# Scores as three f16 products, one product for the last key, and another order of steps in a Perceiver block on one Trainium2 core

## The chip, the core and the metric

The kernel runs on one core of one Trainium2 chip. Four engines take part, each with its own instruction queue: TensorE (PE, matmuls into PSUM), VectorE (DVE), ScalarE (ACT) and GpSimd (POOL); SyncE (SP) issues most of the transfers. The metric is the device time of one execution in microseconds (us), the median of several runs.

## What is computed

The reference takes 64 sequences of 32 tokens (width 256) with 64 contexts of 257 keys (width 128), and adds three layers to the tokens, each behind a layer norm: cross attention, self attention with ternary weights, and a mixture of 8 experts with a capacity of 256 rows each.

```python
x = x + _L0_xattn_ref(_layernorm(x, axis=-1), ctx_1024, Wq, Wk, Wv, Wo, gq, gk)
x = x + _L0_attn_ref(_layernorm(x, axis=-1), w_qkv, w_proj, q_gain)
x = x + _L0_ffn_ref(_layernorm(x, axis=-1), Wg, W1, W3, W2, sw1, sw3, sw2)
# cross attention, 16 heads of width 128
q = rmsnorm((hidden_states @ Wq).reshape(B, Sq, H, D), gq)
k = rmsnorm((encoder_hidden_states @ Wk).reshape(B, Skv, H, D), gk)
scores = jnp.einsum('bqhd,bkhd->bhqk', q, k) * scale
attn = jax.nn.softmax(scores, axis=-1)
out = jnp.einsum('bhqk,bkhd->bqhd', attn, v)
```

## The kernel before

Four sequences (128 tokens) make a tile, and there are 16 tiles. The program is a prologue, a loop of 15 turns, a last part and the experts. A turn of the loop does the cross attention of the next tile up to its probabilities, and everything behind it (the two other layers) of the tile before. The prologue prepares the weights and does the first tile's cross attention; the last part does the late steps of tile 15.

The work of a turn is cut into named steps. Each engine runs its steps in the order of a list (`ORDER`, in the prologue `START_ORDER`), and semaphores tie them: `filled[bank]` counts what TensorE has put in a PSUM bank, `drained[bank]` what has been taken out of it, and a step that writes a bank waits until the one before it there is drained. So the lists and the banks set the order. PSUM is four banks of AB (slots 0 to 3), two of C (4 and 5), Db (D) and Eb (E).

The steps that matter here, with b the sequence of the tile (0 to 3):

- `K0` to `K7`: the keys, of which only the squared norms are wanted. TensorE writes four banks with three products each of f16 halves (`wk_hi`, `wk_lo`, `c_hi`, `c_lo`; high part and remainder). ScalarE squares banks 0 and 1 (`square_keys`, L961), VectorE takes statistics of banks 2 and 3 (`key_stats`, L1345). `KN`, `gKN` and `kn` turn the sums of four steps into inverse norms: VectorE, ScalarE (a logarithm and an exponential as a first guess), VectorE.
- `h` (GpSimd) splits a sequence's context into halves for `K`; `c` and `cl` do so with the rows for `o`.
- `f` closes the cross attention of the tile before (48 products), `Q` makes the queries for their norms (`RQ`, `gRQ`, `rq`), `QP` makes queries times keys' weights, 96 products of f16 halves. ScalarE copies `QP` from AB to `qpT` in f32 (L970) and so drains its banks.
- `rk` (GpSimd, TensorE, ScalarE) spreads the keys' inverse norms, `s` makes the scores: TensorE multiplies `qpT` by `ctxT` in f32, four products of 257 columns (`scores`, L734 to L737), VectorE scales them and takes their maximum (L1513). `e` is the exponential on ScalarE (L1031), `i` the inverse of its sum on VectorE, `n` the normalisation on GpSimd (L1202 to L1212).
- `pt` turns the probabilities on TensorE (`turn_probs`, L739 to L749). The last key doesn't fit in the two blocks of 128; its probabilities stand in `plast`, a row of 12 for each of 4 head groups, and four products with a unit matrix turn them into Db. ScalarE (`ph`, `tl`) and VectorE (`dp`) drain; `o` multiplies with the context rows, `oh` and `do` drain it.
- self attention of the tile before: `xt1`, `qkv`, `gqkv`, `qr` (VectorE, ending with `heads`), `qk` (TensorE turns the heads, ScalarE copies them), `sc` (64 small products), `sm`, `pv`, `st`, `y`, `ys`, `yv`, `pr`; then `ln2`, `xt2`, `lg`, `up`, `dn`, `pos` and `scat`, which sends the rows to the experts.

Of the kernel before, what the change touches and what calls it, by code (L numbers as in the profile page):

```python
# [1791 lines left out]
```

## Time and profile before

| what | value |
|---|---|
| median of 3 runs | 1457.01 us (1456.34 to 1458.7) |
| profiled execution: its time as span | 1457.0 us |
| TensorE busy | 1274.8 us, 87% |
| VectorE busy | 916.5 us, 63% |
| ScalarE busy | 892.3 us, 61% |
| GpSimd busy | 541.9 us, 37% |
| mean granted TensorE clock | 0.954 of full speed |
| prologue, loop, rest | about 0 to 122, 122 to 1277, 1277 to 1457 us |

In a timeline row the columns are the start in the span, the length, the engine, the line of the program, the operation, what is written and read with its shape, and the count; in brackets stands how long the engine sat idle before it and what ended that. A TensorE row's length runs to the end of the pipelined product, so rows overlap and the distance between two starts is what a product costs.

### The profile page before, as it was taken

How to read it: one execution, taken by the hardware profiler on the slowest of the kernel's cores; microseconds unless marked ns; L12 is line 12 of the kernel's file. 1: busy time of each engine (PE TensorE's matmuls, PEld its weight loads, DVE VectorE, ACT ScalarE, POOL GpSimd, SP SyncE). 2: the span in 40 equal slices, each digit the busy share in tenths (PEclk: the TensorE clock that was granted, in tenths of full speed). 3: DMA queues.
4: the chain of work that ended last, by engine and by line, in shares of the span. 5: the costliest groups of instructions: out<-in, count | busy, mean ns of one | idle time of the engine just before them, and what ended most of it. 6: DMA issues, size and time to landing. Idle time of an engine off the chain costs nothing.

```text
span 1457.0 us, 34962 instructions
## 1 busy us (share of the span) xinstructions
PE 1274.8 (87%) x10526; PEld 856.9 (59%) x10526; DVE 916.5 (63%) x3300; ACT 892.3 (61%) x3736; POOL 541.9 (37%) x1337
## 2 busy tenths in 40 slices
PE   5777999999999999999999999999999999846781
PEld 2554666666666666666656566666666666535661
DVE  6744767677676767676767676767666776631212
ACT  4455676767675757585767677676767676611330
POOL 2044252626262534344353525252526262400004
PEclk9998999999999999999999999999999999956986
DMA  9100000101010101010000000000101011003434
...
DMA packets 41183, 59.58 MB, mean 41 GB/s; under 512 B 5094, under 2 KB 35953, under 8 KB 40096
## 3 DMA queue, kind: packets, MB, share of 16 engines
...
q14 instruction: 51, 0.42, 0.1%
q8 instruction: 12, 0.20, 0.1%
...
## 4 chain that ended last, share of the span: by engine, by line
PE 51%; DVE 16%; issue 8%; ACT 8%; POOL 5%; DMA 3%; POOLq 0%; SPq 0%; DVEq 0%; ACTq 0%
PE AB L603 25%; PE Db L603 9%; PE Eb L603 7%; DVE kst L1345 3%; PE C L603 3%; DVE rq L1402 2%; DMA ctxn<-expert_rows 2%; PE C L728 2%; PE C L743 2%; POOL prob L1202 2%; ACT AB L961 1%; ACT prob L1031 1%; DVE pT L1529 1%; DVE px L1611 1%; ACT wt_q L953 1%
## 5 line engine op out<-in xcount | busy, mean ns | idle before, releaser
L961 ACT ACTIVATE AB<-AB 128x128 f32<-128x128 f32 (+1 forms) x1160 | 304.9, 263 | 108.2 <-PE AB L603 105.1
L1157 POOL TENSOR_TENSOR pjunk<-pjunk 128x1 f32<-128x1 f32 x288 | 57.1, 198 | 681.4 <-DVE sinv L1524 387.0
L1345 DVE BATCH_NORM_STATS2 kst<-AB 128x6 f32<-128x256 f32 x512 | 181.7, 417 | 110.1 <-PE AB L603 110.1
L603 PE MATMUL AB<-wk_hi,c_hi 128*128 128x512 f16 x512 | 199.7, 390 | 21.8 <-POOL c_lo L1163 10.0
L961 ACT ACTIVATION_READ_ACCUMULATOR AB<-AB 128x1 f32 (+1 forms) x1160 | 218.1, 188 | 0.0
L603 PE MATMUL AB<-wk_lo,c_hi 128*128 128x512 f16 x512 | 197.8, 386 | 0.0
L603 PE MATMUL AB<-wk_hi,c_lo 128*128 128x512 f16 x512 | 197.3, 385 | 0.0
L1031 ACT ACTIVATE prob<-prob,nbias,rq 128x257 f32<-128x257 f32 x256 | 150.7, 593 | 8.0 <-DVE nbias L1519 8.0
L1202 POOL TENSOR_SCALAR prob<-prob,sinv 128x257 f32<-128x257 f32 x256 | 129.9, 507 | 20.2
L603 PE MATMUL AB<-ctxT,qpT 128*128 128x257 f32 x512 | 123.2, 383 | 11.4 <-ACT pxT L1063 11.4
L603 PEld LDWEIGHTS AB<-wk_hi,c_hi 128*128 128x128 f16 x512 | 50.9, 99 | 103.7 <-issue 32.5
L603 PEld LDWEIGHTS AB<-ctxT,qpT 128*128 128x128 f32 x512 | 92.3, 190 | 26.0 <-ACT pxT L1063 15.5
L1025 ACT COPY rkb<-C 128x512 f32<-128x512 f32 x128 | 69.6, 598 | 56.3 <-PE C L728 55.0
L603 PE MATMUL Eb<-pT,cn_hi 128*128 128x512 f16 x256 | 88.5, 386 | 8.9 <-DVE o_halves L1534 5.1
L1513 DVE CUSTOM_DVE_ANT_0 prob<-AB,rkb 128x257 f32<-128x257 f32 x256 | 94.5, 422 | 0.2
L1529 DVE TENSOR_TENSOR pT<-C,pT 128x512 f16<-128x512 f32 x128 | 82.2, 684 | 13.0 <-ACT pT L1000 12.1
L603 PE MATMUL Db<-wvo_hi,o_halves 128*128 128x256 f16 x512 | 88.8, 276 | 0.7 <-ACT o_halves L993 0.7
L603 PEld LDWEIGHTS AB<-wk_hi,c_lo 128*128 128x128 f16 x512 | 51.0, 100 | 63.4 <-issue 5.3
L603 PE MATMUL AB<-x_hi,wqk_hi 128*128 128x128 f16 x512 | 86.6, 219 | 0.0
L603 PE MATMUL AB<-x_lo,wqk_hi 128*128 128x128 f16 x512 | 86.6, 219 | 0.0
L603 PE MATMUL AB<-x_hi,wqk_lo 128*128 128x128 f16 x512 | 86.6, 219 | 0.0
L743 PE MATMUL C<-consts_sb,prob 128*128 128x128 f32 x512 | 69.0, 278 | 17.5 <-POOL plast L1212 17.4
...
## 6 DMA issues: line engine op xcount, KB each, us to landing
...
ctxn<-in_ctxn SPq DMA_DIRECT2D x64, 128.0 KB, 2.1
...
xin<-in_x SPq DMA_DIRECT2D x16, 128.0 KB, 2.2
prob<-in_wqT SPq DMA_DIRECT2D x1, 2048.0 KB, 19.3
xres<-in_x SPq DMA_DIRECT2D x16, 128.0 KB, 2.0
```

What stands on the lines that cost most here:

```text
L603: return pe.matmul(out, lhsT, rhs, start=start, stop=stop)
L728: ins = pe.transpose(C[:, n, KT * P * (g % 2) + P * tt:KT * P * (g % 2) + P * (tt + 1)], rkx[:, b % 2, tt, P * g:P * (g + 1)], ident)
L743: ins = pe.transpose(C[:, tt, P * g:P * (g + 1)], prob[:, b, g, P * tt:P * (tt + 1)], ident)
L961: ins = nc.scalar.activation(k, k, ACT.Square, accum_out=sums[0:m, h:h + 1])
L1025: nc.scalar.copy(rkb[:, b % 2, 2 * n:2 * n + 2, 0:KT * P], C[:, n].rearrange("p (g n) -> p g n", g=2)).then_inc(drained[s].sem, 1)
L1031: ins = nc.scalar.activation(prob[:, b, g], prob[:, b, g], ACT.Exp, bias=nbias[:, b, g:g + 1], scale=rq[:, G * b + g:G * b + g + 1], accum ...
L1157: own.mark(pool.tensor_tensor(pjunk[:, 0:1], pjunk[:, 1:2], pjunk[:, 1:2], ALU.mult))
L1202: ins = pool.tensor_scalar(prob[:, b, g], prob[:, b, g], sinv[:, b, g:g + 1], P_SCALE, ALU.mult, ALU.mult)
L1345: ins = V.bn_stats(stats[:, 0, 2 * half + n], AB[0:m, 2 + half, 2 * D * n:2 * D * (n + 1)])
L1402: ins = V.tensor_scalar(rq[SQ * m:SQ * (m + 1), G * b:G * (b + 1)], src, 1.0 / WQK_SCALE, None, ALU.mult)
L1513: V.tensor_tensor_reduce(prob[:, b, g], AB[:, g, 0:SKV], rkb[:, b % 2, g], 1.0, BELOW, ALU.mult, ALU.max, smax[:, b, g:g + 1]).then_inc(dr ...
L1529: V.tensor_tensor(pT[:, b % 2, 1, tt], C[:, tt], pT[:, b % 2, 0, tt], ALU.subtract).then_inc(drained[s].sem, 1)
```

## The change

1. **Scores.** `QP` is kept as two f16 halves, `qp_hi` (written by ScalarE) and `qp_lo` (AB minus `qp_hi`, written by VectorE in a new step `QP` that now drains the banks), and a score bank is three f16 products in place of one f32 product. The scale of the weights goes from 1024 to 128.
2. **Last key.** `plast` is 12 numbers per row in place of 4 times 12, one product turns them, and ScalarE writes `pTl` in four instructions with a 0/1 column as scale (`own_group`), which a new reduction in `low` makes.
3. **Order.** The four lists of the loop are replaced; in the prologue only VectorE's list gets `QP`. Each chain of norms gets a buffer of its own (`cube`).

```diff
-WK_SCALE, WQ_SCALE, WQK_SCALE, WVO_SCALE = 64.0, 64.0, 1024.0, 64.0
+WK_SCALE, WQ_SCALE, WQK_SCALE, WVO_SCALE = 64.0, 64.0, 128.0, 64.0
 ORDER = {
-    "PE": """K0 pt3 K1 X K2 o3 K3 f Q xt1 K4 qkv QP rk0 s0 qk sc rk1 K5 K6 K7 pt0 pv s1 st pr rk2 s2 o0 xt2 rk3
-              lg up s3 pt1 dn pos o1 pt2 o2""".split(),
-    "ACT": """K0 tl3 K1 X ph3 K2 oh3 K3 gKN0 Q xt1 gRQ K4 qkv gqkv QP rk0 qk e0 rk1 K5 sc K6 K7 ph0 gKN1 pv tl0
-              rk2 e1 xt2 rk3 oh0 up e2 ph1 lg tl1 e3 oh1 ph2 tl2 oh2""".split(),
-    "DVE": """K0 X K1 XL dp3 K2 K3 KN0 do3 kn0 f Q RQ K4 rq qkv qr s0 sc K5 i0 sm K6 K7 KN1 dp0 kn1 ys yv s1 pr
-              ln2 i1 s2 do0 lg up s3 i2 dn dp1 pos do1 dp2 i3 do2""".split(),
-    "POOL": """h0 n3 h1 X h2 c0 c1 r0 cl ln1 r1 h3 n0 r2 y r3 ln2 c2 n1 c3 n2 scat""".split(),
+    "PE": """K0 K1 pt3 X K2 o3 K3 f Q xt1 K4 qkv rk0 QP qk s0 rk1 sc K5 K6 K7 pt0 pv s1 pr st rk2 s2 o0 xt2 rk3 lg up
+              s3 pt1 dn pos o1 pt2 o2""".split(),
+    "ACT": """K0 K1 X ph3 tl3 K2 oh3 K3 Q gKN0 xt1 gRQ K4 qkv gqkv rk0 QP qk rk1 e0 K5 sc K6 K7 ph0 gKN1 pv tl0 rk2 e1
+              oh0 xt2 rk3 up e2 tl1 ph1 lg e3 oh1 ph2 tl2 oh2""".split(),
+    "DVE": """K0 X K1 XL dp3 K2 do3 K3 KN0 f Q RQ kn0 rq K4 qkv qr QP s0 sc i0 K5 sm K6 K7 KN1 dp0 kn1 ys s1 yv pr ln2
+              s2 do0 i1 lg up i2 s3 dn dp1 pos do1 dp2 i3 do2""".split(),
+    "POOL": """h0 h1 n3 X ln1 h2 r0 r1 cl c2 h3 n0 c0 c3 r2 y r3 ln2 n1 c1 n2 scat""".split(),
 }
...
             def scores(p, b):
                 for g, s in enumerate(BANKS):
                     pe.wait_ge(drained[s].sem, drained[s].turn(p, f"s{b}"))
-                    mm(AB[:, g, 0:SKV], qpT[:, b, P * g:P * (g + 1)], ctxT[:, SKV * b:SKV * (b + 1)])\
-                        .then_inc(filled[s].sem, 1)
+                    rows, keys_ = slice(P * g, P * (g + 1)), slice(SKV * b, SKV * (b + 1))
+                    mm(AB[:, g, 0:SKV], qp_hi[:, b, rows], c_hi[:, keys_], stop=False)
+                    mm(AB[:, g, 0:SKV], qp_hi[:, b, rows], c_lo[:, keys_], start=False, stop=False)
+                    mm(AB[:, g, 0:SKV], qp_lo[:, b, rows], c_hi[:, keys_], start=False).then_inc(filled[s].sem, 1)
...
-                for g in range(G):
-                    ins = mm(Db[0:LK, P * g:P * (g + 1)], plast[:, b, g], ident16[:])
-                ins.then_inc(filled["D"].sem, 1)
+                mm(Db[0:LK, 0:P], plast[:, b], ident16[:]).then_inc(filled["D"].sem, 1)
...
-                    dst = qpT[:, :, 4 * SQ * n:4 * SQ * (n + 1)].rearrange("p b (h q) -> p h b q", q=SQ)
-                    src = AB[:, n].rearrange("p (h b q) -> p h b q", b=NB, q=SQ)
-                    nc.scalar.copy(dst, src).then_inc(drained[s].sem, 1)
+                    nc.scalar.copy(by_batch(qp_hi, n), AB[:, n].rearrange("p (h b q) -> p h b q", b=NB, q=SQ))\
+                        .then_inc(hi_ready.sem, 1)
...
+            def last_probs(p, b):
...
+                act.wait_ge(filled["D"].sem, filled["D"].at(p, f"pt{b}"))
+                for g in range(G):
+                    ins = nc.scalar.activation(pTl[0:LK, b % 2, P * g:P * (g + 1)], Db[0:LK, 0:P], ACT.Copy,
+                                               scale=own_group[0:LK, g:g + 1])
+                ins.then_inc(drained["D"].sem, 1)
...
+            def step_QP(p):
+
+                for n, s in enumerate(BANKS):
+                    dve.wait_ge(hi_ready.sem, hi_ready.at(p, f"QP{s}"))
+                    V.tensor_tensor(by_batch(qp_lo, n), AB[:, n].rearrange("p (h b q) -> p h b q", b=NB, q=SQ),
+                                    by_batch(qp_hi, n), ALU.subtract).then_inc(drained[s].sem, 1)
```

The prologue's list on VectorE reads `... K4 RQ rq wt1 QP M01 wt K5 ...` after the change, where `QP` was not there before.

TensorE, in a turn, from behind the 96 products of `QP` to the first product of `K5`. Before:

```order
L728 MATMUL C<-consts_sb,rkx 128x128 x8
L734 REGISTER_ALU
L603 MATMUL AB<-ctxT,qpT 128x257 x4
L792 REGISTER_ALU
L794 REGISTER_ALU
L796 MATMUL C<-consts_sb,heads 128x128 x8
L801 REGISTER_ALU
L803 REGISTER_ALU
L603 MATMUL AB<-wt_q 32x32 x64
L728 MATMUL C<-consts_sb,rkx 128x128 x8
L618 REGISTER_ALU
L603 MATMUL AB<-wk_hi,c_hi 128x512
```

After (`rk0` now stands ahead of `QP`):

```order
L803 MATMUL C<-consts_sb,heads 128x128 x8
L741 REGISTER_ALU
L610 MATMUL AB<-c_hi,qp_hi 128x257
L610 MATMUL AB<-c_lo,qp_hi 128x257
L610 MATMUL AB<-c_hi,qp_lo 128x257
...
L732 REGISTER_ALU
L735 MATMUL C<-consts_sb,rkx 128x128 x8
L810 REGISTER_ALU
L610 MATMUL AB<-wt_q 32x32 x64
L625 REGISTER_ALU
L610 MATMUL AB<-wk_hi,c_hi 128x512
```

The turn of the heads (`qk`) now stands between `QP` and the scores, and `rk1` ahead of the small products `sc`.

VectorE at the same place, from the last heads to the first scaled scores. Before:

```order
L1582 TENSOR_TENSOR heads<-qk,rot 128x16x16
L1584 TENSOR_TENSOR heads<-qk,rot 128x4x16 x4
L1506 REGISTER_ALU x2
L1510 REGISTER_ALU
L1301 MEMSET junk 128x1
L1513 ISA prob,smax<-AB,rkb 128x257
```

After:

```order
L1605 TENSOR_TENSOR heads<-qk,rot 128x16x16
L1607 TENSOR_TENSOR heads<-qk,rot 128x4x16 x4
L1407 REGISTER_ALU
L1408 TENSOR_TENSOR qp_lo<-AB,qp_hi 128x4x4x32
...
L1529 REGISTER_ALU x2
L1533 REGISTER_ALU
L1316 MEMSET junk 128x1
L1536 ISA prob,smax<-AB,rkb 128x257
```

The subtraction stands there four times, once per bank, between the heads and the scores.

ScalarE at the same place, from the guess for `qkv` to the squares of `K5`. Before:

```order
L1075 ACTIVATE guess_qkv<-guess_qkv 128x20
L967 REGISTER_ALU
L970 COPY qpT<-AB 128x4x4x32 x4
L1024 REGISTER_ALU
L1025 COPY rkb<-C 128x2x256 x2
L952 REGISTER_ALU
L953 COPY wt_q<-C 128x512 x2
L1031 ACTIVATE prob,ssum<-prob,nbias,rq 128x257 x4
L1024 REGISTER_ALU
L1025 COPY rkb<-C 128x2x256 x2
L958 REGISTER_ALU
L961 ACTIVATE AB,kn<-AB 128x128 x8
```

After:

```order
L1091 ACTIVATE guess_qkv<-guess_qkv 128x20
L1040 REGISTER_ALU
L1041 COPY rkb<-C 128x2x256 x2
L974 REGISTER_ALU
L975 CAST qp_hi<-AB 128x4x4x32 x4
L959 REGISTER_ALU
L960 COPY wt_q<-C 128x512 x2
L1040 REGISTER_ALU
L1041 COPY rkb<-C 128x2x256 x2
L1047 ACTIVATE prob,ssum<-prob,nbias,rq 128x257 x4
L965 REGISTER_ALU
L968 ACTIVATE AB,kn<-AB 128x128 x8
```

The exponentials of sequence 0 now stand behind `rk1`, directly ahead of `K5`.

## Rows read from the trace of the kernel before

**Rows 1.** Page, busy time of each engine over the span.
```profile
PE 1274.8 (87%) x10526; PEld 856.9 (59%) x10526; DVE 916.5 (63%) x3300; ACT 892.3 (61%) x3736; POOL 541.9 (37%) x1337
```
**Rows 2.** Timeline of VectorE, step f, which opens the late work of each turn.
```profile
143.54 0.42 DVE L1540 SCALAR_TENSOR_TENSOR x<-Db,xres 128x256 f32<-128x256 f32 x1 [2.30 <-PE Db L603]
...
601.44 0.42 DVE L1540 SCALAR_TENSOR_TENSOR x<-Db,xres 128x256 f32<-128x256 f32 x1 [2.30 <-PE Db L603]
677.29 0.42 DVE L1540 SCALAR_TENSOR_TENSOR x<-Db,xres 128x256 f32<-128x256 f32 x1 [2.30 <-PE Db L603]
754.47 0.42 DVE L1540 SCALAR_TENSOR_TENSOR x<-Db,xres 128x256 f32<-128x256 f32 x1 [2.30 <-PE Db L603]
...
1212.21 0.42 DVE L1540 SCALAR_TENSOR_TENSOR x<-Db,xres 128x256 f32<-128x256 f32 x1 [2.30 <-PE Db L603]
```
**Rows 3.** Table of two stretches: stretch, length, busy time of each engine, granted clock, DMA.
```profile
622.00:626.00 4.00, 4.00 (x63) 2.44 (x51) 2.90 (x8) 3.99 (x20) 0.00 (x0) 1.00 0.00 0
698.00:702.00 4.00, 4.00 (x42) 2.49 (x29) 2.26 (x6) 2.78 (x11) 0.00 (x0) 0.57 0.00 0
```
**Rows 4.** Timeline of TensorE, one turn from Q's end to the next turn's pt3.
```profile
682.27 0.38 PE L612 MATMUL Eb<-consts_sb,xn 128*128 128x128 f32 x2
...
694.72 1.09 PE L796 MATMUL C<-consts_sb,heads 128*128 128x128 f32 x8 [0.22 <-DVE heads L1584]
696.96 1.28 PE L603 MATMUL AB<-wt_q 16*32 16x32 f32 x128 [1.15 <-ACT wt_q L953]
...
699.73 0.63 PE L603 MATMUL AB<-wk_hi,c_hi 128*128 128x512 f16 x1
...
711.33 2.00 PE L603 MATMUL AB<-ctxT,qpT 128*128 128x257 f32 x8 [0.76 <-ACT pxT L1063]
...
735.03 0.39 PE L603 MATMUL AB<-wk_hi,c_hi 128*128 128x512 f16 x1 [0.67 <-POOL c_lo L1163]
...
738.18 1.09 PE L743 MATMUL C<-consts_sb,prob 128*128 128x128 f32 x8 [0.38 <-POOL plast L1212]
```
**Rows 5.** Chain that ended last, three pieces on TensorE (start, length, what).
```profile
672.01 5.24 PE Db L603 x48
...
724.26 1.74 PE AB L603 x8
...
726.87 0.32 PE Db L603 x4
```
**Rows 6.** Timeline of VectorE in the same turn.
```profile
684.63 1.42 DVE L1345 BATCH_NORM_STATS2 kst<-AB 128x6 f32<-128x256 f32 x4 [0.69 <-PE AB L603]
...
693.97 0.62 DVE L1584 TENSOR_TENSOR heads<-qk,rot 128x64 f32<-128x64 f32 x4
...
696.21 0.16 DVE L1519 SCALAR_TENSOR_TENSOR nbias<-smax,rq 128x4 f32<-128x4 f32 x1 [0.22 <-DVE smax L1513]
...
711.65 0.22 DVE L1320 SCALAR_TENSOR_TENSOR nc_<-guess_KN 128x64 f32<-128x64 f32 x1
...
729.05 1.28 DVE L1529 TENSOR_TENSOR pT<-C,pT 128x512 f16<-128x512 f32 x2
```
**Rows 7.** Timeline of ScalarE in the same turn.
```profile
697.59 0.59 ACT L1031 ACTIVATE prob<-prob,nbias,rq 128x257 f32<-128x257 f32 x1
...
701.25 0.26 ACT L961 ACTIVATE AB<-AB 128x128 f32<-128x128 f32 x1 [0.69 <-PE AB L603]
...
703.51 0.62 ACT L1038 ACTIVATE px<-sc 128x512 f32<-128x512 f32 x1
```
**Rows 8.** Prologue, timelines of TensorE (step M01) and of VectorE (its remainder).
```profile
59.76 3.67 PE L603 MATMUL AB<-pxT,pT 128*128 128x256 f32 x16
...
64.28 2.48 DVE L1427 SCALAR_TENSOR_TENSOR wvo_lo<-AB,wvo_hi 128x512 f16<-128x512 f32 x4
```
**Rows 9.** Last part: a piece of the chain that ended last, and VectorE's timeline.
```profile
1272.05 0.57 ACT pTl L953
...
1314.32 0.48 DVE L1621 SCALAR_TENSOR_TENSOR x<-Eb,rstd,x 128x256 f32<-128x256 f32 x1 [3.46 <-PE Eb L603]
```

More of the change, by code:

```diff
@@ L163 @@
     "ACT": """KL K0 wq0 K1 wq1 K2 X K3 gKN0 rkl Q W0a W0b W1a W1b K4 gRQ QP M0a M0b K5 M1a M1b tw rk0 e0 rk1 e1 K6 ph0 tl0 K7 gKN1 ph1 tl1 oh0 rk2 e2 rk3 oh1 e3 ph2 tl2 oh2""".split(),
-    "DVE": """low wk KL KNL K0 K1 X K2 XL wql K3 gg KN0 kn0 Q W0l wt0 W1l K4 RQ rq wt1 M01 wt K5 M23 tw s0 s1 i0 K6 dp0 i1 K7 KN1 kn1 do0 dp1 s2 s3 i2 dp2 do1 i3 do2""".split(),
+    "DVE": """low wk KL KNL K0 K1 X K2 XL wql K3 gg KN0 kn0 Q W0l wt0 W1l K4 RQ rq wt1 QP M01 wt K5 M23 tw s0 s1 i0 K6 dp0 i1 K7 KN1 kn1 do0 dp1 s2 s3 i2 dp2 do1 i3 do2""".split(),
     "POOL": """hl h1 h3 h2 h0 rkl X r0 r1 cl c0 n0 c1 n1 r2 c2 r3 n2 c3""".split(),
@@ L328, in build @@
         guess = {n: sb(f"guess_{n}", [P, k]) for n, k in (("KN0", NB * H), ("KN1", NB * H), ("RQ", H), ("qkv", NQK))}
-        nc_ = sb("nc_", [P, NB * H])
+        cube = {n: sb(f"cube_{n}", [P, k]) for n, k in (("KN0", NB * H), ("KN1", NB * H), ("RQ", H), ("qkv", NQK))}
         tscale = sb("tscale", [P, 10], BF16)
@@ L392, in build @@
                              last=["gqkv"])
-        high_steps = ["wq0", "wq1", "W0a", "W0b", "W1a", "W1b", "M0a", "M0b", "M1a", "M1b", "X"]
-        hi_ready = Events(sem("hi_ready"), pro=steps_among("ACT", PRO, high_steps), full=["X"])
+        high_steps = ["wq0", "wq1", "W0a", "W0b", "W1a", "W1b", "M0a", "M0b", "M1a", "M1b", "X", "QP"]
+        parts = {"QP": [f"QP{s}" for s in BANKS]}
+        hi_ready = Events(sem("hi_ready"), pro=[n for s in steps_among("ACT", PRO, high_steps) for n in parts.get(s, [s])],
+                          full=[n for s in steps_among("ACT", FULL, high_steps) for n in parts.get(s, [s])])
         rkx_ready = Events(sem("rkx_ready"), pro=["last"] + entries("POOL", PRO, "r"), full=entries("POOL", FULL, "r"))
@@ L453, in build @@
         eo = [flat_view(oT[:, 4 * k:4 * k + 4], "p a n", 2) for k in range(2)]
-        fin = [x[:, :].rearrange("p b n -> p (b n)").rearrange("p (a c) -> p a c", c=DIM) for x in
-               (qpT, rkx[:].rearrange("p a k n -> p (a k) n"))]
-        fin = [f[:, 4 * k:4 * k + 4] for f in fin for k in range(2)]
+        fin = [x[:, :].rearrange("p b n -> p (b n)").bitcast(F32).rearrange("p (a c) -> p a c", c=DIM) for x in (qp_hi, qp_lo)]
+        fin += [rkx[:].rearrange("p a k n -> p (a k n)")[:, 1024 * k:1024 * (k + 1)].rearrange("p (a c) -> p a c", c=DIM)
+                for k in range(2)]
         got = [pxT[:, 2 * n:2 * n + 2, :].rearrange("p a n -> p (a n)") for n in range(8)]
@@ L1000, in probs_high @@
                     nc.scalar.copy(pT[:, b % 2, 0, tt], C[:, tt]).then_inc(ph_ready[tt].sem, 1)
+            def last_probs(p, b):
+                if p.kind == "pro":
+                    act.wait_ge(start_dve.sem, start_dve.at(p, "low"))
+                act.wait_ge(filled["D"].sem, filled["D"].at(p, f"pt{b}"))
[3 more added lines that the diff above has]
+                ins.then_inc(drained["D"].sem, 1)
             def wqk_high(p, k, half):
@@ L1205, in normalise @@
                 own.settle()
-                rows = plast[:, b].rearrange("p g r -> p (g r)")
-                diag = [rows[:, G * e:G * e + 1 + (LK + 1) * (G - 1):LK + 1] for e in range(3)]
+                part = [plast[:, b, G * e:G * (e + 1)] for e in range(3)]
                 last = prob[:, b, :, SKV - 1]
-                own.mark(pool.tensor_tensor(diag[0], last, ones[:, 0:G], ALU.mult))
+                own.mark(pool.tensor_tensor(part[0], last, ones[:, 0:G], ALU.mult))
                 own.settle()
-                own.mark(pool.tensor_tensor(diag[1], last, ones[:, 0:G], ALU.mult))
-                pool.tensor_tensor(diag[2], last, diag[0], ALU.subtract).then_inc(p_ready.sem, 1)
+                own.mark(pool.tensor_tensor(part[1], last, ones[:, 0:G], ALU.mult))
+                pool.tensor_tensor(part[2], last, part[0], ALU.subtract).then_inc(p_ready.sem, 1)
             def split_rows(p, b):
@@ L1307, in newton @@
                 for r in range(3):
-                    c = nc_[0:rows, 0:n]
+                    c = cube["KN1"][0:rows, 0:n]
                     step(V.scalar_tensor_tensor(c, w, -0.5, w, ALU.mult, ALU.mult))
@@ L1671, in step_dn @@
                 V.tensor_tensor(base[:], x2[:], Eb[:, 0:DIM], ALU.add).then_inc(drained["E"].sem, 1)
[L1673 removed]
+            steps = dict(X=step_X, XL=step_XL, Q=lambda p: key_stats(p, "Q", P, qst), RQ=step_RQ, QP=step_QP,
                          wql=step_wql, W0l=lambda p: step_Wl(p, 0), W1l=lambda p: step_Wl(p, 1), f=step_f, qkv=step_qkv, sc=step_sc, sm=step_sm, ys=step_ys, yv=step_yv,
```

14 lines of the change are left out of this document (9 added, 5 removed).

## The prediction

> **What bounds the kernel now.** I read the page first, then the timeline of each engine over one turn of the loop, the chain of waits, and last the prologue and the last part. On the page TensorE is busy for 87% of the span and no other engine for more than 63% [rows 1]. That invites the thought that each microsecond taken from TensorE is one of the kernel's, and the turn shows how far it is so.
>
> The loop's pace is read from one VectorE step that every turn has once [rows 2]. From 143.54 to 1212.21 there are 14 turns, 76.33 us each. They are of two kinds: 601.44 to 677.29 is 75.85, 677.29 to 754.47 is 77.18. What parts them is TensorE's clock. In the shorter turn it is granted in full from 622 to 626; at the same place of the longer one (698 to 702) it is 0.57, so most of that stretch runs at 1.2 in place of 2.4 GHz [rows 3], and `K5` starts there with products 0.43 us apart. Ahead of both lies a thin stretch: TensorE waits for the heads, then 1.15 us for their copies, and then only has small products [rows 4]. The mean turn lies 0.48 above the short kind, so about a third of the turns (5 of 14) pay the 1.33.
>
> I cut the turn at four places of TensorE [rows 4]: the end of `Q` at 682.27, `K5` at 699.73, the scores of sequence 1 (`s1`) at 711.33 and the next turn's `K0` at 735.03. From `Q` to `s1` it is 29.06, and 27.73 without the slow stretch; from `s1` to `K0` 23.70; so 24.42 is left from `K0` to the next `Q`'s end.
>
> **What the change takes from TensorE.** A score step takes 1.74 now, four f32 products of 257 columns. The new one has twelve f16 products, and f16 products of 256 columns follow each other in 5.24/48 = 0.109 [rows 5], so 1.31: 0.43 saved, 1.7 a turn. Turning the last key takes 0.32 for four products, and 0.08 for one: 0.24 saved, 1.0 a turn. Together 2.7 a turn, 40 us over 15 turns. The rest of the working asks how much of it reaches the end.
>
> **From K0 to Q's end.** `K0` and `K1` now stand ahead of `pt3`, and GpSimd splits both before it normalises. `K1` covers the 0.38 that `pt3` waited for GpSimd [rows 4], with some 0.17 more because a row's length hides the first part of a wait. With 0.24 of the last key: **0.8 saved**. On ScalarE the four instructions of `tl` come to at most 4 x 0.26 [rows 7] against 0.57 [rows 9]; 0.5 more for each of four is hidden here, since ScalarE idles between blocks.
>
> **From Q's end to s1**, counted from 682.27. Here the lists matter more than the products.
> - VectorE finished the heads at 694.59, that is 12.3 [rows 6]. Its new list puts `kn0` (three instructions of 0.22 with their waits, 0.7) ahead of `rq`, and takes back the 0.69 it idled for `K4`, now behind `rq`. The heads stay at 12.4.
> - TensorE ends `QP` at 10.3 (`rk0` ahead of it, scores gone from behind it) and then has `qk` next. The scores, 1.74 of work that covered the wait for the heads, are now behind it. So it stands for some 2.2 in place of 0.22.
> - `QP`'s low half is four new VectorE instructions. Two of the same form and size take 1.28 [rows 6], so four take 2.5. They stand behind the heads and ahead of the scaled scores, and each bank of scores waits for its own: banks come free at 13.1, 13.7, 14.3 and 14.9, and TensorE's shorter scores gain nothing.
> - VectorE then scales them; from the heads to the bias (696.21) this took 1.6 to 1.8. So the bias is at 16.5, and the small products `sc` at 16.5 in place of 14.7. `rk1` (0.87) is now ahead of them, in the gap. `K5` starts at about 18.1: 1.2 for `sc` and 0.3 until VectorE has drained the first bank. Undisturbed it was 16.8. **1.3 lost.**
> - ScalarE had done the exponentials `e0` during `sc`. Now it copies `rk1` until 16.9, does `e0` in 4 x 0.59 [rows 7] until 19.3, and only then the squares of `K5`. Eight squares take 703.51 - 701.25 = 2.26, and the exponential of `sc` 0.62: the squares of `K7` end at 19.3 + 3 x 2.26 + 0.62 = 26.7. TensorE's blocks of 2.6 wait for these drains, some 0.8 in all. From `K7`'s end at 26.7 to `s1` there are a turn of probabilities, `pv` and its copies, 2.3. `s1` comes at 29.0 in place of 27.73. **1.3 lost** in all from `Q` to `s1`.
>
> The new VectorE step has the whole queue behind it: scaled scores, `sc`, the sum of exponentials. Unknown is how far ScalarE is really late. Its bounds: nothing is lost behind `K5` (then 1.3 falls to 1.0) and `e0` a further 0.6 late (1.9).
>
> **From s1 to K0.** Three score steps and two turns are shorter by 3 x 0.43 + 2 x 0.24 = 1.8. `K0` waits for GpSimd (0.67 [rows 4]), which sends the expert rows first; that needs VectorE's `pos` behind `s3` and `dp1`. VectorE now takes `i2`, which waits for `e2`, before `s3`; this holds `s3` for about a microsecond. Bounds are 0 and 1.8 saved; I take **0.7**, because the first half of this leg follows TensorE and the second follows ScalarE and VectorE.
>
> **Sum for a turn:** 75.85 - 0.8 + 1.3 - 0.7 = 75.6 undisturbed. The thin stretch grows from about 3.5 to 8 us with some 3 us of standing still, so I expect half clock in two turns of three up to all. A slow stretch costs less there, 1.0 to 1.3, since ScalarE holds `K5` to `K7` anyway. Taken at 0.85 a turn: 76.45, 0.1 above 76.33, **+2 us** in 15 turns. The Trainium skill ("TensorE: Matmul & The Clock Gate", What's actually happening) says that the default state is throttled and activity releases the throttle. By that rule all 15 turns would pay, which is 75.6 + 1.2 = 76.8 and +7; the trace agrees in that the two stretches just read differ so.
>
> **Prologue.** VectorE is its chain here. `M01` started at 59.76, right behind `QP`, with its remainders at 64.28 [rows 8], just as VectorE came free. Now `M01` needs banks that VectorE drains from 64.3 on, 0.6 apart; 3.67 of products follow from 65.0, then ScalarE's high half (1.0), and the remainders end near 71.0 in place of 66.8: **+4**. Bounds: 2.5 (only the new work) and 5.
>
> **Last part.** `ph3` is now ahead of `tl3`, whose 0.57 stood ahead of the last attention [rows 9]: 1.3 saved. `pr` is ahead of `st`, and VectorE's wait of 3.46 for it shrinks by 1.2. **-2.5**, between 0 and -4.
>
> **Total:** 1457.0 + 2 + 4 - 2.5 = 1460.5. The profiled span, 1457.0, is the median of the runs, so nothing is converted. 0.2% (2.9 us) is what a measurement can tell from no change.
>
> **Rivals.**
> 1. **The other side: `K5` to `K7` are not held by ScalarE, and the clock stays.** Then the loss to `s1` is 1.0, the last leg saves 1.3, and the dips stay at a third: 75.85 - 0.8 + 1.0 - 1.3 = 74.75, plus 0.45; 75.2 a turn is -17, with prologue and last part 1441. For it: ScalarE is 61% busy [rows 1]. Against: `e0` now stands directly ahead of `K5`. It decides at `e0` ending before 18.9, when `K5`'s first bank is full. Chance 0.30.
> 2. **TensorE's saving arrives whole:** 1457 - 40 + 1.5 = 1418. This needs the low halves hidden, but they stand ahead of scores that need them. Chance 0.06.
> 3. **The clock falls in every turn and ScalarE is 0.6 later:** 75.6 + 1.3 + 0.6 = 77.5, +17, total 1476. For it: 2.2 us of standing where 0.22 was. Chance 0.14.
> 4. **The change adds nothing anywhere:** the new products cost what the old did and the lists even out, 1457. It is in the forecast's range.
>
> **How the numbers follow.** The forecast has 0.50, with 1452 to 1470 as its own range: leg bounds of 0.3 up and down over 15 turns are 5, prologue and last part 3. The range that should hold 8 in 10 takes in most of rival 1 and part of 3: 1439 to 1473. Faster by over 0.2%: rivals 1 and 2 whole, and a little of the forecast, 0.37. Within: 0.20. Slower: 0.43.
>
> **What would show it.** TensorE should stand for about 2 us between `QP` and `qk`, scores should come in four pieces about 0.6 apart, `sc` 16.5 behind `Q`'s end and `s1` 29.0. The last leg should read 23.0, and `pt3` should not wait. The twelve score products should still be 0.109 apart in `s1` to `s3`. The granted clock should read about 0.57 behind `sc` in most turns. In the prologue the first `rk0` should come 4 us later. I am wrong if the turn lies under 75.5, which the leg from `Q` to `s1` would show first, or if the new subtraction takes much other than 0.62.

## The result and the profile after

| what | value |
|---|---|
| after, median of 4 runs | 1525.34 us (1523.67 to 1530.42) |
| before, median of 4 runs beside them | 1457.12 us (1456.34 to 1458.7) |
| ratio | 1.0474, 95% interval 1.0455 to 1.0493: slower |
| profiled execution after | span 1530.3 us, mean granted clock 0.938 |

The forecast was 1460.5 with 1439 to 1473 as its range. The size was missed by 65 us. The sign was the one given the larger chance (0.43 against 0.37), but what decided it was nothing that the forecast had counted, so that it came out is luck.

The page of after, beside [rows 1]: busy time of each engine, the chain that ended last by engine and by line, and one group of instructions.

```profile
PE 1268.4 (83%) x10590; PEld 851.9 (56%) x10590; DVE 997.8 (65%) x3365; ACT 916.6 (60%) x3928; POOL 536.3 (35%) x1337
...
PE 48%; DVE 22%; issue 9%; ACT 6%; DMA 3%; POOL 3%; DVEq 1%; POOLq 0%; SPq 0%; ACTq 0%
PE AB L610 29%; PE Db L610 8%; DVE rq L1424 6%; PE Eb L610 5%; ACT prob L1047 3%; DVE kst L1360 2%; DMA ctxn<-expert_rows 2%; PE C L735 2%; DVE prob L1536 1%; PE C L610 1%; DVE qp_lo L1408 1%; DVE pT L1552 1%; PE C L752 1%; DVE rqt L1337 1%; PE C L803 1%
...
L1424 DVE TENSOR_SCALAR rq<-rqt 32x4 f32<-32x4 f32 x256 | 99.0, 387 | 3.8
```

TensorE is only 6 us less busy, VectorE 81 more. About 40 of these are the new `qp_lo` (2.48 sixteen times). More than the rest stands in the last row: `rq`, sixteen small moves a tile of the same form as before, now has 6% of the chain and 387 ns a move in the mean, where it had 160 (99.0 us in all in place of about 41).

**Where the 73 us between the two spans are.** Step `f` [rows 2] marks the turns; here are two of its rows after.

```profile
640.32 0.42 DVE L1563 SCALAR_TENSOR_TENSOR x<-Db,xres 128x256 f32<-128x256 f32 x1 [3.67 <-PE Db L610]
...
721.73 0.42 DVE L1563 SCALAR_TENSOR_TENSOR x<-Db,xres 128x256 f32<-128x256 f32 x1 [3.66 <-PE Db L610]
```

The first `f` comes at 154.38 in place of 143.54 (10.8 in the prologue), the next fourteen turns take 80.77 each in place of 76.33 (62.1 in all), and what is left behind the fifteenth `f` takes 0.4 more. The loop made the loss.

The same four places of TensorE as in [rows 4], in the turn that holds 721.73.

```profile
726.71 0.38 PE L619 MATMUL Eb<-consts_sb,xn 128*128 128x128 f32 x2
...
737.52 0.29 PE L610 MATMUL AB<-x_hi,wqk_hi 128*128 128x128 f16 x1 [3.00 <-DVE kst L1360]
...
743.49 1.09 PE L803 MATMUL C<-consts_sb,heads 128*128 128x128 f32 x8 [1.62 <-DVE heads L1607]
744.41 0.27 PE L610 MATMUL AB<-c_hi,qp_hi 128*128 128x257 f16 x1
...
747.61 1.28 PE L610 MATMUL AB<-wt_q 16*32 16x32 f32 x128 [0.42 <-DVE smax L1536]
...
749.23 0.39 PE L610 MATMUL AB<-wk_hi,c_hi 128*128 128x512 f16 x1 [0.34 <-DVE sc L1614]
...
760.06 0.28 PE L610 MATMUL AB<-c_hi,qp_hi 128*128 128x257 f16 x1 [0.82 <-ACT pxT L1079]
...
783.34 0.39 PE L610 MATMUL AB<-wk_hi,c_hi 128*128 128x512 f16 x1 [0.99 <-POOL c_lo L1179]
```

From `Q`'s end (726.71) `sc` is 20.9 away (forecast 16.5), `K5` 22.5 (18.1), `s1` 33.4 (29.0); from `s1` to `K0` it is 23.3 (23.0), from `K0` to the next `Q`'s end 23.8 (23.6). Each piece is within 0.3 except the first, so all of it is lost between `Q` and `sc`. TensorE already stands 3.00 inside `QP`, for statistics of `K4` that VectorE has behind `rq`. VectorE and GpSimd in that stretch:

```profile
729.36 0.65 DVE L1337 SCALAR_TENSOR_TENSOR rqt<-cube_RQ,guess_RQ 128x16 f32<-128x16 f32 x1
730.04 6.63 DVE L1424 TENSOR_SCALAR rq<-rqt 32x4 f32<-32x4 f32 x16
736.71 1.42 DVE L1360 BATCH_NORM_STATS2 kst<-AB 128x6 f32<-128x256 f32 x4
...
743.28 2.48 DVE L1408 TENSOR_TENSOR qp_lo<-AB,qp_hi 128x512 f16<-128x512 f32 x4
```

```profile
729.38 1.15 POOL L1209 COPY rkx<-rk 128x512 f32<-128x512 f32 x2
...
730.75 1.16 POOL L1209 COPY rkx<-rk 128x512 f32<-128x512 f32 x2
...
732.00 0.60 POOL L1247 CAST cl_cast<-ctxl 12x512 f16<-12x512 f32 x1
732.68 1.03 POOL L1249 TENSOR_TENSOR cl_cast<-cl_cast,low_rows 12x512 f16<-12x512 f16 x1
733.79 1.14 POOL L1252 TENSOR_TENSOR cl_rows<-ctxl,cl_cast 12x512 f16<-12x512 f32 x1
```

GpSimd's block `r0 r1 cl c2 h3` runs from 729.1 to 737.4, `rq` from 730.0 to 736.7. Before, GpSimd did nothing while `rq` ran. All instances of `rq` on one line (shortest, median, longest in ns), before and then after:

```profile
L1402 DVE TENSOR_SCALAR rq<-rqt x256: 156/160/167, 57.0 to 1224.1; 32x4 f32<-32x4 f32 x128
```

```profile
L1424 DVE TENSOR_SCALAR rq<-rqt x256: 157/295/1036, 60.0 to 1299.8; 32x4 f32<-32x4 f32 x128
```

The shortest is the same; the longest, 1.04 us, is about as long as GpSimd's longest instructions here (1.03 to 1.16). That reads like a move that waits until a GpSimd instruction is over. The theory for the experiments: VectorE and GpSimd exclude each other, and the loss is that the new lists (`kn0` late, so `r0` starts with `rq`) put them side by side. The rivals: the products and step `QP` cost it, or the lists by their order alone.

### The profile page after: what moved, and what is told of

Read it like the earlier page. It is cut to its first block, busy times and chain, and to the rows that moved or that the text cites. A ratio compares the mean times of both kernels' runs of the same rounds, so it can differ in the third digit from the quotient of the medians.

```text
span 1530.3 us, 35395 instructions
## 1 busy us (share of the span) xinstructions
PE 1268.4 (83%) x10590; PEld 851.9 (56%) x10590; DVE 997.8 (65%) x3365; ACT 916.6 (60%) x3928; POOL 536.3 (35%) x1337
## 4 chain that ended last, share of the span: by engine, by line
PE 48%; DVE 22%; issue 9%; ACT 6%; DMA 3%; POOL 3%; DVEq 1%; POOLq 0%; SPq 0%; ACTq 0%
PE AB L610 29%; PE Db L610 8%; DVE rq L1424 6%; PE Eb L610 5%; ACT prob L1047 3%; DVE kst L1360 2%; DMA ctxn<-expert_rows 2%; PE C L735 2%; DVE prob L1536 1%; PE C L610 1%; DVE qp_lo L1408 1%; DVE pT L1552 1%; PE C L752 1%; DVE rqt L1337 1%; PE C L803 1%
## 5 line engine op out<-in xcount | busy, mean ns | idle before, releaser
L968 ACT ACTIVATE AB<-AB 128x128 f32<-128x128 f32 (+1 forms) x1160 | 298.4, 257 | 128.6 <-PE AB L610 126.1
L610 PE MATMUL AB<-wk_hi,c_hi 128*128 128x512 f16 x512 | 197.2, 385 | 27.8 <-POOL c_lo L1179 12.4
L968 ACT ACTIVATION_READ_ACCUMULATOR AB<-AB 128x1 f32 (+1 forms) x1160 | 212.8, 183 | 0.0
L610 PE MATMUL AB<-x_hi,wqk_hi 128*128 128x128 f16 x512 | 106.1, 243 | 45.0 <-DVE kst L1360 45.0
L1193 POOL TENSOR_TENSOR rstd<-var,minus_half 128x1 f32<-128x1 f32 x64 | 35.5, 555 | 302.0 <-DVE var L1345 255.4
L1218 POOL TENSOR_SCALAR prob<-prob,sinv 128x257 f32<-128x257 f32 x256 | 123.7, 483 | 20.2
L610 PE MATMUL AB<-x_lo,wqk_hi 128*128 128x128 f16 x512 | 106.1, 243 | 0.0
L610 PE MATMUL AB<-x_hi,wqk_lo 128*128 128x128 f16 x512 | 106.0, 243 | 0.0
L1424 DVE TENSOR_SCALAR rq<-rqt 32x4 f32<-32x4 f32 x256 | 99.0, 387 | 3.8
L1552 DVE TENSOR_TENSOR pT<-C,pT 128x512 f16<-128x512 f32 x128 | 82.2, 682 | 10.8 <-ACT pT L1006 9.9
L610 PE MATMUL Db<-wvo_hi,o_halves 128*128 128x256 f16 x512 | 86.5, 273 | 0.7 <-ACT o_halves L999 0.7
L610 PE MATMUL AB<-c_hi,qp_hi 128*128 128x257 f16 x256 | 72.4, 283 | 13.3 <-ACT pxT L1079 12.3
```

Of the source, the lines that this page charges most:

```text
L610: return pe.matmul(out, lhsT, rhs, start=start, stop=stop)
L968: ins = nc.scalar.activation(k, k, ACT.Square, accum_out=sums[0:m, h:h + 1])
L1193: pool.tensor_tensor(rstd[:, n:n + 1], var[:, n:n + 1], minus_half[:], ALU.pow)\
L1218: ins = pool.tensor_scalar(prob[:, b, g], prob[:, b, g], sinv[:, b, g:g + 1], P_SCALE, ALU.mult, ALU.mult)
L1424: ins = V.tensor_scalar(rq[SQ * m:SQ * (m + 1), G * b:G * (b + 1)], src, 1.0 / WQK_SCALE, None, ALU.mult)
L1552: V.tensor_tensor(pT[:, b % 2, 1, tt], C[:, tt], pT[:, b % 2, 0, tt], ALU.subtract).then_inc(drained[s].sem, 1)
```

## Experiments

Each run has one edit or one group of them, and the numbers in the headings are used as names below. "Before" was run beside each, at 1449 to 1461 us; a ratio is to that. "Turn" is the mean of the fourteen turns of the loop in the profiled execution.

**1. `rq` by another kind of instruction.** In the changed kernel (the factor 1/128 goes into the squares before):

```diff
-  ins = V.tensor_scalar(rq[...], src, 1.0 / WQK_SCALE, None, ALU.mult)
+  ins = V.tensor_reduce(rq[...], src.unsqueeze(2), AX.X, ALU.add)
```

> The changed kernel, but the sixteen small moves of step rq are reductions over an axis of one element (the factor 1/128 goes into the squares before), everything else in place. Rival A (the new step QP and the three products cost the 4.4 a turn wherever rq stands): unchanged, 1525. Rival B (every small VectorE instruction is slower beside GpSimd, whatever its kind): rq stays near 6.6 and the whole at 1525.

1502.07 us, ratio 1.0336 (1.0308 to 1.0365), turn 79.05, where 1462 and 76.5 were expected. The instances of `rq`:

```profile
L1424 DVE TENSOR_REDUCE rq<-rqt x256: 145/150/156, 55.4 to 1266.9; 32x4 f32<-32x4 f32 x128
```

Not one is held up, beside the same GpSimd block, so rival B falls. But only about a third of the loss is gone. Two things took much of the rest. The instructions behind `rq` now meet the block (0.85 and 0.61 for what took 0.20 and 0.17, and a third that took 0.54 in place of 0.18):

```profile
715.01 0.85 DVE L1573 COPY vals<-qkv 128x64 f32<-128x64 f32 x1
...
716.82 0.61 DVE L1576 TENSOR_SCALAR squares_qkv<-qkn 128x20 f32<-128x20 f32 x1
```

And TensorE's standstill moved from inside `QP` to behind it, right ahead of `qk` and the scores, where the clock then was granted at half, 1.2 of 2.4 GHz:

```profile
721.79 1.83 PE L803 MATMUL C<-consts_sb,heads 128*128 128x128 f32 x8 [3.71 <-DVE heads L1607]
723.42 0.42 PE L610 MATMUL AB<-c_hi,qp_hi 128*128 128x257 f16 x1
```

```profile
722.00:725.00 3.00, 3.00 (x16) 0.50 0.00 0
```

**2. `kn0` back ahead of `f`** in the changed kernel's VectorE list, `gKN0` ahead of `Q` on ScalarE.

```diff
-    "DVE": ... KN0 f Q RQ kn0 rq K4 ...        "ACT": ... Q gKN0 xt1 ...
+    "DVE": ... KN0 kn0 f Q RQ rq K4 ...        "ACT": ... gKN0 Q xt1 ...
```

> The changed kernel with kn0 put back ahead of f on VectorE, and its first guess ahead of Q on ScalarE. GpSimd's list is untouched, but its r0 no longer waits for a late kn0. Theory: GpSimd starts r0 some 4 us sooner, right behind h2, and is near the end of its 8.3 us of work when rq begins, so half to all of the extra in rq goes; 2 to 4 us a turn, the whole 1465 to 1495, less what then collides with f and RQ. Rivals: no instruction was taken away, so 1525 within 5.

1499.65 us, ratio 1.0307 (1.0276 to 1.0339), turn 79.07, 5 us above the expected range. `rq` fell to 3.71 in the turn read, but the block now met the small steps of `RQ` and the first of `rq`, three of which took 0.57, 0.90 and 0.70 in place of 0.17:

```profile
558.24 0.90 DVE L1414 TENSOR_SCALAR squares_RQ<-qn 128x16 f32<-128x16 f32 x1
...
560.90 3.71 DVE L1422 TENSOR_SCALAR rq<-rqt 32x4 f32<-32x4 f32 x16
```

**3. Only `kn0` late, in the kernel before**, with f32 scores and no `QP`.

```diff
-    "DVE": ... do3 kn0 f Q RQ K4 rq ...   "ACT": ... gKN0 Q ...   "POOL": ... c1 r0 cl ln1 r1 ...
+    "DVE": ... do3 f Q RQ kn0 K4 rq ...   "ACT": ... Q gKN0 ...   "POOL": ... c1 ln1 r0 cl r1 ...
```

> The kernel before, with f32 scores and no step QP; only kn0 moved behind RQ on VectorE, its guess behind Q on ScalarE, and GpSimd's ln1 ahead of r0. Theory: GpSimd's r0, cl, r1 and h3 (about 5.8 us) now run beside rq, whose single moves go from 0.16 to 0.3 to 0.5 in the mean, rq takes 5 to 6.5, and the turn grows by 2.5 to 4: 1495 to 1517. Rivals A (products) and the order of VectorE alone: within 5 of 1457.

1519.14 us, ratio 1.0446 (1.0401 to 1.049), turn 80.59, 2 us above the expected range. The loss is there without any of the new products. `rq` in a turn, and GpSimd beside it:

```profile
723.20 5.98 DVE L1400 TENSOR_SCALAR rq<-rqt 32x4 f32<-32x4 f32 x16
```

```profile
723.21 1.05 POOL L1232 TENSOR_TENSOR cl_cast<-cl_cast,low_rows 12x512 f16<-12x512 f16 x1
724.34 1.14 POOL L1235 TENSOR_TENSOR cl_rows<-ctxl,cl_cast 12x512 f16<-12x512 f32 x1
```

`rq` alone is 3.2 of the 4.3 that a turn takes more. The rest isn't taken apart: `kn0` (0.7) now stands ahead of `rq` as well, and the granted clock is under full in all fourteen turns, before in five.

**4. All four new lists, old products.** The kernel before with the changed lists, less `QP` on VectorE.

> The kernel before with the lists of the changed one on all four engines and without QP on VectorE: f32 scores, four products for the last key. Theory: rq is as slow as in the changed kernel (6.6), the heads 4.3 later; without QP's 2.5 on VectorE, sc is about 1 us sooner than there, the later scores 0.4 each longer: 79.5 to 81 a turn, 1505 to 1530. Rival A (products cost it): 1457 to 1465.

1535.1 us, ratio 1.0567 (1.0534 to 1.06), turn 81.91, 5 us above the expected range: the lists alone cost even more than the whole change. Rival A isn't needed for a loss of this size; whether the products cost something of their own is the next run's question.

**5. All new products, old lists,** with `QP` between `qr` and `s0` on VectorE.

> All products, halves and the last key as in the changed kernel, but the four lists of before, with QP on VectorE between the heads and s0. Nothing of GpSimd then runs beside rq. Theory (the lists cost it, by putting GpSimd's block beside rq and the scores behind the heads): rq 2.8, no long standstill of TensorE ahead of the heads; QP's 2.5 on VectorE against 2.7 saved on TensorE leaves 75 to 77 a turn, 1440 to 1465. Rival A (the products and QP cost it): 1490 to 1525.

1521.55 us, ratio 1.045 (1.042 to 1.0481), turn 80.2. Here the theory was wrong by some 60 us: `rq` is at 156/160/167 again and it is as slow. Two waits of TensorE over the loop (in all, times, longest), and the second of them in the kernel before:

```profile
PE AB L607 <- DVE qp_lo L1405: 37.2, 15, 2.5
PE AB L607 <- ACT wt_q L957: 16.4, 15, 1.2
```

```profile
PE AB L603 <- ACT wt_q L953: 16.9, 15, 1.2
```

The old list has the scores ahead of `qk`; they wait 2.5 a turn for the low half, a wait that wasn't there before, and `qk` and `sc` stand behind them, where `sc` still waits for `wt_q` as it did. That wait is 37 of the 59 us that the fifteen turns take more. The rest isn't taken apart; the clock has a part in it, under full in all fourteen turns. So with the old lists the new products lose as much in another way, and they need a new TensorE list; what they don't need is the collision that came with it.

**6. The changed kernel without the collision:** run 2, and GpSimd's whole list as before.

> The changed kernel with kn0 ahead of f as in the run before (1500), and GpSimd's whole list as it was before, so that its block is done when rq begins. TensorE's list stays the new one, with the scores behind qk. Theory: RQ and rq lose the 2.9 us that they still paid in that run; TensorE stands 2 to 3 us ahead of the heads as there and may fall to 1.2 GHz. 76 to 77.5 a turn, 1455 to 1478. Rival B (what is left of the loss has nothing to do with GpSimd): 1495 to 1505.

1468.63 us, ratio 1.0082 (1.0052 to 1.0112), turn 76.82. 57 of the 68 us are gone, by the order of steps on VectorE, ScalarE and GpSimd alone. Rival A falls with this as the cause of the loss in the changed kernel. The forecast, which left the collision out, describes this kernel. `rq` is at 156/160/167, and the pieces of one turn (TensorE, then VectorE):

```profile
620.08 0.38 PE L617 MATMUL Eb<-consts_sb,xn 128*128 128x128 f32 x2
...
636.63 1.28 PE L608 MATMUL AB<-wt_q 16*32 16x32 f32 x128 [0.42 <-DVE smax L1534]
...
638.25 0.39 PE L608 MATMUL AB<-wk_hi,c_hi 128*128 128x512 f16 x1 [0.34 <-DVE sc L1612]
...
649.08 0.28 PE L608 MATMUL AB<-c_hi,qp_hi 128*128 128x257 f16 x1 [0.80 <-ACT pxT L1077]
...
672.26 0.39 PE L608 MATMUL AB<-wk_hi,c_hi 128*128 128x512 f16 x1 [0.72 <-POOL c_lo L1177]
```

```profile
622.92 2.77 DVE L1422 TENSOR_SCALAR rq<-rqt 32x4 f32<-32x4 f32 x16
...
631.75 0.63 DVE L1605 TENSOR_TENSOR heads<-qk,rot 128x64 f32<-128x64 f32 x4
```

**7, 9, 10. The last key and the harmless part of the lists, old scores.** 7: the kernel before with one product for the last key. 9: 7, with `K0 K1 pt3` on TensorE, `K0 K1 X ph3 tl3` on ScalarE, `h0 h1 n3` on GpSimd. 10: 9, with `pr st`, `s1 yv`, and `oh0` and `tl1` earlier.

> The kernel before with its lists and its f32 scores; only the last key's turn is new: one product, and four scaled copies on ScalarE. TensorE saves 0.24 four times a turn, ScalarE takes 0.5 more four times. By the legs that follow TensorE it is 0.3 to 0.8 a turn less, 1445 to 1452 where before is 1457; if ScalarE's longer step is on the path behind the scores, no gain or up to 5 more.

> The kernel with the old scores and only the new last key (1450.5), and of the new lists only K1 ahead of pt3 on TensorE, ph3 ahead of tl3 on ScalarE, h1 ahead of n3 on GpSimd. Expected from the legs: 0.4 a turn less because pt3 no longer waits for GpSimd, 1443 to 1447; no gain (1449 to 1452) if the leg from K0 to Q follows VectorE or ScalarE.

> As the one before, and also pr ahead of st on TensorE, s1 ahead of yv on VectorE, and oh0 and tl1 ahead as in the new ScalarE list; kn0, GpSimd's block and the scores stay where they were. Expected: a further 0 to 0.3 a turn and 1 to 3 us in the last turn and the last part, 1438 to 1446; slower than the run beside it if s1 ahead of yv delays pr.

7: 1450.5 us, ratio 0.9966 (0.9951 to 0.998), turn 75.85. 9: 1437.28 us, 0.9884 (0.9856 to 0.9912), turn 75.29. 10: 1439.48 us, 0.9874 (0.9849 to 0.9898), turn 75.36, no different from 9. 9 is 13 under 7, where 4 to 7 was expected: 8 in the fourteen turns, and 5 in the one behind them. Between turns at full clock 9 gains 0.34, about the 0.4 expected; the rest in the turns is that three of fourteen had the clock under full in 7 and one in 9. In the turn behind them 2.4 of the 5 are the closing products of `f` (7.79 in 7, 5.43 in 9), which ran at full clock only in 9.

**8, 12. The prologue, and `h1` first, in kernel 6.** 8: `QP` ahead of `wt1` in VectorE's prologue. 12: 8, with `h0 h1 n3`.

> The kernel of the run that gave 1468.6 (changed products, kn0 and GpSimd's list put back), and in the prologue VectorE takes QP ahead of wt1 in place of behind it. Theory (in the prologue TensorE stands 5 us for qp_lo and then runs M01 at 1.2 GHz): M01 starts some 4 us sooner, the remainders of wvo wait for VectorE's own wt1 instead; 2 to 4 us off the first f, whole 1464.5 to 1467. Rival (the loss in the prologue sits in the twelve score products or elsewhere behind the weights): unchanged, 1468.6.

> The changed products with kn0 and GpSimd's list put back and the prologue mended (1462.9), and of the new GpSimd list only h1 ahead of n3, which was worth 13 in the kernel with the old scores (1450.5 to 1437.3) and which that kernel lacked. Theory (all that the change loses is the block beside rq and the late banks of the prologue; the products are worth about nothing by themselves): 1449 to 1455, that is up to 0.5% under before and 12 over the kernel with old scores. If the products pay at last, under 1440; if their standing still ahead of the heads costs more, over 1456.

8: 1462.91 us, ratio 1.0035 (1.0017 to 1.0053), somewhat more than the expected gain; the first `f` at 148.3 in place of 153.9, of which 0.8 was gained before `rq` already; the turns as in 6. 12: 1464.74 us, 1.0065 (1.0046 to 1.0083), turn 76.81 as in 8: nothing gained, where 1449 to 1455 was expected. So `h1` first is worth nothing in this kernel. That points at the two other edits of 9, `K1` ahead of `pt3` on TensorE and `ph3` ahead of `tl3` on ScalarE, which kernel 6 had already; no run has them one at a time.

**11, 13, 14, 15. `rq` on GpSimd.** The sixteen moves become a step of GpSimd behind `h3`, sixteen `tensor_tensor` by a column of ones, each waiting for the one before.

```diff
+  for b in range(NB):
+      for m in range(4):
+          own.settle()
+          ins = pool.tensor_tensor(rq[...], src, ones[SQ * b:SQ * (b + 1), 0:G], ALU.mult)
```

11: in kernel 9, with `qk` ahead of `s0`. 13: in kernel 12. 14: in the changed kernel with its own lists. 15: in kernel 9, lists kept.

> The kernel of old scores and best lists (1437.3), with rq's sixteen moves on GpSimd, one after another, and qk ahead of s0 on TensorE. Theory: in this stretch VectorE's queue sets the heads, so 2.8 us off it bring qk ahead of the scores without a standstill and hide ScalarE's copies of its result: 1.0 to 1.5 a turn, 1415 to 1423. Against: GpSimd's moves are now the ones beside VectorE's small steps; if each holds up one, or nbias waits for the sixteenth, 1437 or more.

> The kernel of the first run of this group (changed products, all mended), with rq's moves on GpSimd. Theory: the heads come 2.8 sooner, TensorE no longer stands ahead of them and keeps its clock, QP's low half starts when ScalarE's high half allows: 1 to 2 us a turn, 1420 to 1437. If ScalarE's copies of QP then hold VectorE, only 0.5 a turn, 1440 to 1448.

> The changed kernel with its own four lists and one edit: rq's sixteen moves leave VectorE and are the next step of GpSimd behind its block. Theory (a collision needs both engines): the 6.6 us on VectorE go whole; GpSimd ends its block near 10.7 behind Q's end and the moves near 15.3, just before nbias wants them; single VectorE steps beside the block still lose 1 to 2 us. The turn falls from 80.8 to 74.5 to 77, the whole to 1432 to 1470. If the block slows whatever stands on VectorE just as much, 1490 or more.

> The kernel of old scores and best lists (1437.3) with rq on GpSimd and TensorE's list left alone, so that the scores still stand ahead of qk. There TensorE reached the heads within 0.2 us of their being ready, so VectorE's 2.8 us should be worth next to nothing: 1432 to 1438. If it comes out under 1425, the old scores are as good as the new products (1422.6) and these are worth nothing.

| kernel | us | ratio to before, interval | turn |
|---|---|---|---|
| 11 old scores, `qk` first | 1456.68 | 1.0008 (0.9992 to 1.0024) | 76.35 |
| 13 new products, mended lists | 1422.62 | 0.9768 (0.9744 to 0.9792) | 73.87 |
| 14 changed kernel, one edit | 1460.19 | 1.0025 (1.0006 to 1.0044) | 76.41 |
| 15 old scores, `rq` on GpSimd | 1431.71 | 0.9826 (0.9806 to 0.9846) | 75.07 |

14 is the change as it is, with one step moved to another engine, and 65 us less. 13 is the best kernel found, 2.3% under before. Against 12 it has only `rq` on GpSimd, and its turn is 2.94 shorter. 0.5 of this is the clock: in 12 seven of the fourteen turns have it under full (77.34 in the mean, the others 76.27), in 13 none. The other 2.4 are most of the 2.77 that `rq` takes on VectorE: with the products new and nothing colliding, VectorE's queue from `RQ` to the heads sets this stretch. Its rows, VectorE and GpSimd, then TensorE:

```profile
675.38 1.43 DVE L1374 BATCH_NORM_STATS2 kst<-AB 128x6 f32<-128x256 f32 x4
677.50 0.20 DVE L1582 COPY vals<-qkv 128x64 f32<-128x64 f32 x1 [0.69 <-ACT qkv L959]
```

```profile
675.81 4.53 POOL L1222 TENSOR_TENSOR rq<-rqt,ones 32x4 f32<-32x4 f32 x16
```

```profile
672.66 0.38 PE L618 MATMUL Eb<-consts_sb,xn 128*128 128x128 f32 x2
...
682.99 1.04 PE L802 MATMUL C<-consts_sb,heads 128*128 128x128 f32 x8
...
686.99 1.28 PE L609 MATMUL AB<-wt_q 16*32 16x32 f32 x128 [0.43 <-DVE smax L1545]
```

TensorE has no wait for the heads left, and `sc` is 14.3 behind `Q`'s end. GpSimd needs longer for the moves (0.28 each) but in the loop nobody waits for them. 11 missed its forecast by 34 or more: the f32 scores end late behind `qk`, `sc` waits 1.3 for VectorE's maxima, and it comes 15.0 behind `Q`'s end and `s1` 29.4, where 15 has 14.2 and 27.4. 15 is 5.6 under 9, at the edge of what was expected, and 9 over 13. That is what the new scores with their lists are worth against the old scores with theirs, once `rq` is on GpSimd in both; the lists of the two differ, so not all of it need be the scores.

## Why the prediction was wrong, and where it was right

**The step that failed is "The heads stay at 12.4"**, in the part on VectorE from `Q`'s end to `s1`. In the changed kernel they end 16.65 behind `Q`'s end (743.36 - 726.71). The step counted how many instructions stood ahead of the heads and took `rq` as long as before. `kn0` was priced as 0.7 of VectorE's time, not as the signal that lets GpSimd begin `r0`. I did look at GpSimd's list for `K0` and `pt3`, but not at what its moved block would run beside. Run 6, where nothing collides, gives the heads 12.3 behind `Q`'s end (632.38 - 620.08), `sc` 16.6 (forecast 16.5), `K5` 18.2 (18.1), `s1` 29.0 (29.0), and `s1` to `K0` 23.2 (23.0). In the changed kernel `rq` took 3.86 more and `rqt` 0.48 more, and these 4.3 went down the chain unshortened: the turn that was read is 4.4 longer than the one of run 6, and the mean turn 3.9 (half of run 6's turns have a stretch under full clock, see below). That the collision does this is shown from both sides: run 6 takes it away, run 2 in part, run 14 takes `rq` out of it, and 3 brings it into the old kernel. Run 1 shows that it hangs on the kind of instruction.

It could have been seen before. One line of the trace of before, the same instruction at three durations:

```profile
L1334 DVE TENSOR_SCALAR xn<-x,mv,rstd x32: 412/612/1504, 146.3 to 1316.3; 128x256 f32<-128x256 f32 x32
```

412 ns is its own time; 1504 is what it took while GpSimd copied `rkx`. The Trainium skill ("SBUF — State Buffer", Who interferes with whom) says that VectorE shares one of its two pairs of ports with GpSimd under an exclusive lock held for a whole instruction, that `tensor_scalar`, copies and casts on VectorE can want that pair, that instructions with two SBUF inputs contend with a GpSimd instruction that reads SBUF, and that `tensor_reduce` never contends on this chip. The runs agree at each point where they can: `tensor_scalar` 157 to 1036 ns, `tensor_reduce` 145 to 156 beside the same block, and in run 14 the two-input `heads` (128x256) up to 779 where it had 424. The rule spoke against this change, and I did not set it beside the new lists.

**Turn by turn.** Run 6 has a mean turn of 76.82 against the 76.45 forecast, and the 0.4 between them is two errors against each other. Seven of its fourteen turns have the clock under full, in turn with the others (the length stands second, the clock third from the end):

```profile
615.10:691.10 76.00, 69.61 (x635) 45.81 (x634) 55.51 (x203) 54.47 (x241) 32.30 (x83) 1.00 0.07 21
691.10:768.63 77.53, 71.06 (x635) 47.00 (x634) 55.61 (x203) 54.55 (x241) 32.49 (x83) 0.98 0.07 21
```

The seven at full clock take 76.0 to 76.5, mean 76.3, where 75.6 was forecast: 0.7 too little. The other seven take 1.1 more, 0.5 a turn over all, where 0.85 was forecast: 0.3 too much. The forecast's "two turns of three up to all" was too many for this kernel. In the changed kernel all fourteen turns have the clock under full, but in the turn that was read the stretch stood in `QP` (0.66 from 738 to 742) and not behind `sc`; the standstill ahead of it had moved there too. These rows are of the changed kernel, the first from its prologue:

```profile
68.00:72.00 4.00, 3.90 (x10) 0.57 0.00 0
738.00:742.00 4.00, 3.87 (x46) 0.66 0.00 0
```

**The prologue** was sized at +4, bounds 2.5 and 5, and measured +10.8, so this term was mis-sized as well. 3.0 of it is there before `rq` begins (59.99 against 57.02), where the kernels differ by one small reduction; over the runs this start lies anywhere between 55.1 and 60.1, also without the change (59.9 in run 3), so I don't count it as the change's. From there to the first `f` it is +7.9 (94.4 against 86.5). I had the standstill for the banks (counted from `rq`'s start `M01` comes 5.4 later, forecast 5.2), but took `M01` at full clock:

```profile
68.10 5.16 PE L610 MATMUL AB<-pxT,pT 128*128 128x256 f32 x15 [4.90 <-DVE qp_lo L1408]
```

```profile
67.27 2.48 DVE L1408 TENSOR_TENSOR qp_lo<-AB,qp_hi 128x512 f16<-128x512 f32 x4
72.86 1.29 DVE L1449 SCALAR_TENSOR_TENSOR wvo_lo<-AB,wvo_hi 128x512 f16<-128x512 f32 x2 [3.11 <-ACT wvo_hi L992]
```

After 4.90 of standing it ran at 0.57 and took 5.2 in place of 3.7. With that the last remainder of this group ends 6.2 later in place of 4.2; the 1.7 that are added up to the first `f` aren't taken apart. Run 8 takes the standstill away and is 4.8 shorter from `rq` to the first `f` than run 6 (89.4 and 94.2); run 12, with the same lists in the prologue, has 87.4.

**The rest.** Last part -2.5: behind the fifteenth `f` the changed kernel has +0.4, but its last turn still has the collision; run 6 has -5.5. Right were the new subtraction (2.48 for four), the twelve score products 0.11 apart, and `pt3` not waiting. The scores of sequence 0 do come in four pieces, but 0.34, 0.46 and 0.60 apart (744.41, 744.75, 745.21, 745.81), since TensorE comes to them when the first banks are already free. The forecast had the new arithmetic and lists come out even in a turn (0.8 and 0.7 saved, 1.3 lost). Once `rq` is out of VectorE's queue, part of the 2.7 gets through: run 13's turn is 1.2 shorter than that of run 15, which has the old scores and `rq` on GpSimd too, though its lists differ as well. Rival 1 had the right direction for that, but not its means. None of the four rivals had the collision. It belonged there as the one on the slower side, with its price from the `xn` row.
